# Feed-forward loop of a macaron block: both code planes of quantised x made by GpSimd instead of VectorE

## The reference

```
x = x + 0.5 * ffn(layernorm(x)); x = x + attn(layernorm(x)); x = x + 0.5 * ffn(layernorm(x))
ffn(x):  gate = q(x) @ q(w_gate).T; y = q(x) @ q(w_up).T; h = silu(gate) * y; return q(h) @ q(w_down).T
q(x):    per block of 16: scale = max|x| / 6; x / scale rounded to a grid of 8 magnitudes and sign, times scale
```

## Time and profile before

| what | us |
|---|---|
| median of three runs (lowest, highest) | 1416.26 (1414.32, 1421.88) |
| profiled execution, own time | 1417.98 |
| its span, first to last instruction | 1416.2 |
| busy in the span: TensorE, VectorE, ScalarE, GpSimd | 1258.7, 1160.1, 728.3, 578.6 |
| granted TensorE clock, mean | 0.981 of full |

### The profile page before, as it was taken

One profiled execution on the slowest core, in us unless ns is written; L12 is line 12 of the kernel. 1 busy time (PEld: TensorE's weight loads), 2 busy tenths in 40 slices (PEclk: granted clock), 3 DMA queues, 4 the chain that ended last, 5 costly groups with the idle time before them and its releaser, 6 DMA issues.

```text
span 1416.2 us, 28364 instructions
## 1 busy us (share of the span) xinstructions
PE 1258.7 (89%) x9008; PEld 820.2 (58%) x9008; DVE 1160.1 (82%) x3635; ACT 728.3 (51%) x1473; POOL 578.6 (41%) x530
## 2 busy tenths in 40 slices
PE   0669999999998699989998999899999999999997
PEld 0236555555555476767676677667755555555555
DVE  5689999999998686668667766676489999999997
ACT  3456666666653343424342443444276666666653
POOL 1144444445543244324332434244245444555542
PEclk9889999999999999999999999899999999999999
DMA  9524444444444000000000000000035444455555
GB/s 320 95 57 84 83 84 79 79 79 79 83 84 80 30 2 1 1 32 2 1 1 32 1 2 1 31 9 9 1 64 105 101 101 101 103 106 106 106 106 117
DMA packets 284583, 90.55 MB, mean 64 GB/s; under 512 B 263120, under 2 KB 283728, under 8 KB 284496
## 3 DMA queue, kind: packets, MB, share of 16 engines
q1 hardware_dynamic: 276752, 81.56, 27.9%
q10 hardware_dynamic: 7744, 7.86, 1.8%
HBM read 11.34 MB, written 8.39 MB: 14 GB/s over the span
## 4 chain that ended last, share of the span: by engine, by line
PE 31%; DVE 27%; issue 26%; POOL 8%; ACT 5%; DMA 1%; DVEq 1%; ACTq 0%; SPq 0%; POOLq 0%
PE ps L1378 12%; PE ps L1399 9%; DVE arena L833 4%; DVE arena L893 4%; POOL arena L461 4%; PE ps L1388 3%; PE ps L1358 3%; POOL arena L450 2%; DVE arena L837 2%; PE ps L1365 2%; DVE arena L822 2%; ACT arena L576 2%; ACT arena L615 2%; DVE arena L782 2%; DVE arena L846 1%
## 5 line engine op out<-in xcount | busy, mean ns | idle before, releaser
L1330 PE MATMUL ps<-wguT,arena 128*128 128x512 f16 (+1 forms) x2304 | 482.7, 364 | 26.4 <-DVE m_sb L1262 14.0
L1330 PEld LDWEIGHTS ps<-wguT,arena 128*128 128x128 f16 x2304 | 226.3, 98 | 251.2 <-issue 32.9
L461 POOL TENSOR_TENSOR arena<-arena 128x704 f32<-128x704 f32 x128 | 192.4, 1503 | 347.7 <-DVE arena L846 340.4
L1302 PE MATMUL ps<-wdT,arena 128*128 128x256 f16 x2176 | 262.3, 275 | 60.2 <-DMA arena<-arena 59.9
L1302 PEld LDWEIGHTS ps<-wdT,arena 128*128 128x128 f16 x2176 | 205.1, 98 | 125.1 <-issue 74.9
L483 POOL TENSOR_TENSOR arena<-arena 128x128 f16<-128x128 f32 (+7 forms) x64 | 143.9, 2249 | 239.0 <-ACT arena L680 239.0
L622 ACT ACTIVATE arena<-arena 128x704 int16<-128x704 f32 x128 | 100.8, 787 | 216.5 <-POOL arena L461 216.5
L1378 PE MATMUL ps<-arena 128*128 128x512 f16 (+2 forms) x960 | 194.1, 356 | 0.0
L1399 PE MATMUL ps<-arena 128*128 128x256 f16 x1632 | 191.8, 273 | 0.0
L672 ACT ACTIVATE arena<-ps,arena,cst 128x128 f32<-128x128 f32 (+7 forms) x64 | 80.4, 1257 | 183.9 <-DVE arena L1003 183.9
L1399 PEld LDWEIGHTS ps<-arena 128*128 128x128 f16 x1632 | 157.5, 98 | 22.7 <-issue 0.9
(11 more groups left out here) (126 smaller groups left out, 1675.2 us busy)
## 6 DMA issues: line engine op xcount, KB each, us to landing
out_dram<-x_sb SPq DMA_DIRECT2D x32, 256.0 KB, 2.7
x_sb<-in_L_attn_x_dram ACTq DMA_DIRECT2D x3, 2048.0 KB, 17.8
arena<-arena SPq DMA_TRANSPOSE x192, 3.5
arena<-arena SPq DMA_DIRECT2D x8, 256.0 KB, 2.8
arena<-arena SPq DMA_DIRECT2D x4, 512.0 KB, 4.2
x_sb<-in_L_attn_x_dram ACTq DMA_DIRECT2D x1, 1536.0 KB, 7.4
arena<-in_L_ffn_w_down_dram SPq DMA_DIRECT2D x1, 704.0 KB, 8.3
arena<-in_L_ffn_w_gate_dram SPq DMA_DIRECT2D x1, 640.0 KB, 4.5
```

Source lines behind the costliest of these rows:

```text
L461: g.tensor_tensor(hy[u].rearrange("p (j b) -> p b j", j=BL), h[u].rearrange("p (b j) -> p b j", j=BL), hri[u].unsqueeze(2).to_broadcast([P ...
L1302: i = nc.tensor.matmul(ps_dn[w % 2], hT[w][:, c * P:(c + 1) * P], wdT[:, k, :], start=(s == 0), stop=(s == len(DOWN_STEPS) - 1))
L1330: i = nc.tensor.matmul(psf[:, 1536 * u + lo:1536 * u + hi], xv[:, u, xl, kt, :], wguT[:, wl, lo // P:hi // P, kt, :], start=(s == 0), stop ...
```

## The change

GpSimd gets the two instructions that make `xq`. Its list of a pair becomes: `pool_h_y` first half, plane 0 of x, `pool_h_y` second half, plane 1 of x, `pool_x_y`, `pool_x_rstd`. VectorE loses both `dve_x_q` in the loop and keeps them for the first pairs of each phase, which are prepared in the head of the program and in the attention part. `x_q` now counts both planes (two for each pair), SyncE waits for `2 * q + 2`, and VectorE's `dve_x_sh` waits in addition until GpSimd has made both planes of the pair before, since it overwrites `xsh`. `act_*`, TensorE's list and the order of SyncE's list stay as they are.

```diff
         def sp_x_T(q, par):
-            nc.sync.wait_ge(x_q, q + 1)
+            nc.sync.wait_ge(x_q, 2 * q + 2)
...
+        def pool_x_q(q, pl, done=None):
+            g = nc.gpsimd
+            if pl == 0:
+                g.wait_ge(x_g, q + 1)
+                if done is not None:
+                    g.wait_ge(x_T[done[1]], done[0] * 16 + 16)
+            g.wait_ge((x_sh, x_sl)[pl], q + 1)
+            s = (xsh, xsl)[pl].rearrange("p (t b) -> p t b", t=2)
+            g.tensor_tensor(xq.rearrange("p (t l j b) -> p l t j b", t=2, l=2, j=BL)[:, pl],
+                            xg.rearrange("p (t j b) -> p t j b", t=2, j=BL),
+                            s.unsqueeze(2).to_broadcast([P, 2, BL, XB]), ALU.mult).then_inc(x_q, 1)
...
         def dve_x_sh(q):
             V.wait_ge(x_sd, q + 1)
+            if not isinstance(q, int) or q >= 1:
+                V.wait_ge(x_q, q * 2)
...
                 dve_h_sh(n, u)
-                if early:
-                    dve_x_q(gp + 2, 0, (qd + odd, 1 - odd))
                 dve_h_sl(n, u)
-                if early:
-                    dve_x_q(gp + 2, 1)
```

More of the change, by code:

```diff
@@ L501, in macaron_block_kernel, with pool_pair @@
         X_SLOT = (3, 6, 9, 12)
-        def pool_pair(gp, odd, x3=True, x4=True):
+        def pool_pair(gp, qd, odd, x2=True, x3=True, x4=True):
             pool_h_y(2 * gp, 0)
+            if x2:
+                pool_x_q(gp + 2, 0, (qd + odd, 1 - odd))
             pool_h_y(2 * gp + 1, 1)
+            if x2:
+                pool_x_q(gp + 2, 1)
             if x3:
@@ L553, in _ @@
                     continue
-                pool_pair(first, 0)
-                pool_pair(first + 1, 1)
+                pool_pair(first, first // 2, 0)
+                pool_pair(first + 1, first // 2, 1)
                 with pool.Fori(0, (NP - 6) // 2) as i:
-                    pool_pair(i * 2 + (first + 2), 0)
-                    pool_pair(i * 2 + (first + 3), 1)
+                    pool_pair(i * 2 + (first + 2), i + (first // 2 + 1), 0)
+                    pool_pair(i * 2 + (first + 3), i + (first // 2 + 1), 1)
                 for k in range(NP - 4, NP):
-                    pool_pair(first + k, k % 2, x3=(k < NP - 3), x4=(k < NP - 4))
+                    pool_pair(first + k, (first + k) // 2, k % 2, x2=(k < NP - 2), x3=(k < NP - 3), x4=(k < NP - 4))
                     if not first and k == NP - 3:
@@ L821, in dve_x_q @@
             s = (xsh, xsl)[pl].rearrange("p (t b) -> p t b", t=2)
[L822 to L826, removed]
+            V.tensor_tensor(xq.rearrange("p (t l j b) -> p l t j b", t=2, l=2, j=BL)[:, pl],
+                            xg.rearrange("p (t j b) -> p t j b", t=2, j=BL),
+                                s.unsqueeze(2).to_broadcast([P, 2, BL, XB]), ALU.mult).then_inc(x_q, 1)
         def dve_h(n, u):
```

## The result

The change makes the kernel slower: 1473.24 us (median of four runs, 1472.25 to 1476.35) against 1417.89 (1414.32 to 1421.88), ratio 1.0393, 95% interval 1.0359 to 1.0427. The forecast was 1462, with a range of 1403 to 1490.

What follows compares the result with a forecast made beforehand. It took the loop's path through VectorE, GpSimd and ScalarE as the bound. One stretch growing from 5.37 to 6.12 us gave +0.75 us a pair, times 60 pairs +45 us, so 1462 us, range 1403 to 1490.

Steps and rivals of the forecast that it cites:

- the give-back of the path ahead of GpSimd's recorded end: Path shared by VectorE and GpSimd: GpSimd gives it up about 0.14 us ahead of its instruction's end.
- The first rival: At plane 0 GpSimd loses the race, or little is lost: -14 us, far end -39 us; chance 0.17.
- the second: Rival: only plane 0 collides and `dve_x_s` is not held at plane 1: +0.17 us a pair, +10 us; chance 0.10.
- The third: Rival: GpSimd's planes hold the path from start to end: +1.09 us a pair, +65 us; chance 0.15.
- The other half of that reading: Path shared by VectorE and GpSimd: GpSimd needs it only from about 0.14 us behind its instruction's start.
- the 5.37 us: Stretch of a pair from the end of `dve_x_g` to the end of `pool_x_y`, forecast to become 6.12: +0.75 us.
- the rival walk in which nobody is held: Far end of the faster rival: small VectorE instructions never wait, `pool_x_y` ends at 4.72: -0.65 us a pair; chance 0.05.

Runs made afterwards that it cites:

- `tiny_planes`: The changed kernel, with each plane GpSimd makes in the loop cut to 4 of its 512 columns; waits and order kept: 1381.24 us, ratio 0.9722.
- `late_transpose`: The kernel before the change, with SyncE also waiting for the next pair's `pool_x_y` ahead of the transpose of x: 1423.91 us, ratio 1.0021.
- `plane0_after_hg`: The changed kernel, with GpSimd also waiting for `dve_h_g` of the same place ahead of plane 0: 1460.74 us, ratio 1.0291.
- `both_early`: Both planes on GpSimd between the two products of h, VectorE's x steps moved ahead of `dve_h_rin`: 1440.6 us, ratio 1.0139.
- `reorder_only`: The kernel before, planes on VectorE, with first-half `dve_x_sh`, `dve_x_c` and `dve_x_g` moved ahead of `dve_h_rin`: 1413.37 us, ratio 0.9959.

## Why the prediction was right

The direction and the mechanism were right, and the size was 10 us short: +55 us measured (58.4 between the two profiled executions) against +45. Point by point, in us from the end of `dve_x_g`, for the pair that was walked:

| step | predicted | measured |
|---|---|---|
| plane 0, start and end | 0.16, 1.29 | 0.23, 1.38 |
| `dve_h_rin` starts (1.29 before) | 1.50 | 1.60 |
| second product of h | 2.00 to 3.50 | 2.09 to 3.59 |
| plane 1 | 3.45 to 4.52 | 3.45 to 4.61 |
| `dve_x_s` comes, `dve_x_rin` starts | 3.79, 4.58 | 3.89, 4.68 |
| `pool_x_y` ends (5.37 before) | 6.12 | 6.18 |
| from there to the next end of `dve_x_g` | 6.70 | 6.69 |

Who goes first was called right at both places inside the loop: `dve_h_sl` still gets in, `dve_h_s` is held, `dve_x_s` is held. So was the give-back of the path ahead of GpSimd's recorded end: take its own 0.18 us off the end of `dve_h_s`, and it ran from 1247.77, 0.13 ahead of the plane's end; `dve_x_s`, with 0.17, ran from 1251.00, again 0.13 ahead. The first rival (GpSimd loses, faster) needed `dve_h_s` at 0.18 us and showed 1.16; the second (`dve_x_s` not held) was refuted at 0.76. (In that first walk `dve_x_s` comes at 2.92 and not at 2.96, which changes nothing.) The third (held from start to end) comes to 6.44 for the end of `pool_x_y` with the planes where they really ran: plane 0 until 1.38, `dve_h_rin` at 1.73, plane 1 until 4.74, `dve_x_rin` at 4.94 and 1.50 from there. Measured 6.18.

The other half of that reading, that GpSimd needs the path only from 0.14 us behind its start, isn't confirmed, and that `dve_h_sl` got in doesn't speak for it: plane 0 started at 0.23 and not at the predicted 0.16, so `dve_h_sl` at 0.15 was first in any case. Outside the loop plane 0 starts earlier, 0.07 to 0.09 behind `dve_x_g`, and there, in seven pairs, it is `dve_h_sl` (L897) that is held:

```profile
1078.72 1.16 POOL L464 TENSOR_TENSOR arena<-arena 128x512 f16<-128x512 f16 x1 [3.06 <-DVE arena L830]
1078.79 1.15 DVE L897 TENSOR_TENSOR arena<-arena 128x44 f16<-128x44 f32 x1
```

It starts 0.07 us behind the plane; if the plane left the path free for 0.14, it would have got in. In the loop, `dve_h_sl` is 0.08 ahead, and neither is longer for the 0.12 us in which their records overlap (0.20 and 1.15). So when GpSimd takes the path stays open. The sum hardly depends on it, since either order holds one short VectorE instruction until the plane ends.

Three terms were mis-sized. First, the walk came out 0.06 us short. Plane 0 started 0.07 later than predicted and ran 1.15 us where 1.13 had been reckoned (1.07 and a wait of 0.06), so the steps behind it came 0.09 to 0.10 late. Plane 1 took 1.16 in place of 1.07 (the f16 difference of attention in the earlier trace rows, 1.16, was the nearer row and not `pool_x_y`), but it started 0.14 ahead of the end of the product before it in place of 0.05, and so added nothing. And `pool_x_y` followed `dve_x_rin` 0.04 sooner than reckoned. Second, the 5.37 us are those of one half of the loop's body. In the other half the same stretch was 5.28 us (from 1214.52 to the end of `pool_x_y` at 1219.80), and it is 6.17 now. So one pair loses 0.81, the other 0.89, 0.85 on average, and 60 times that is 51 us. Third, the prediction said that the two `dve_x_q` were 0.86 us of the path; the rival walk in which nobody is held had `dve_h_rin` going from 1.29 to 0.63 without them, and `tiny_planes` shows 0.64. The right figure is 0.65, since one of them filled the time in which `dve_h_sl` waits for `dve_h_sh`. That sentence didn't enter the sum. Of the 58.4 us between the profiled executions 53.4 lie in the feed-forward phases, so 2 us there are left over, mostly in the pairs outside the loop; 4.1 lie in the attention part, where they differ from one execution to another, and 0.9 in the head.

TensorE behaved as told: it waits ahead of the gate product, 35.2 us in 23 waits of 2.0 us at most between 1100 and 1400 us, and no VectorE or ScalarE row shows the lateness. `late_transpose` shows that such waits are free here.

The Trainium skill, "SBUF — State Buffer", section "Who interferes with whom", has whoever issues first hold the path for the whole instruction. The exclusion agrees with every row above. By the recorded times the hold ends before the instruction does: a hold to the recorded end would have put the end of `pool_x_y` at 6.44, measured 6.18, and the held VectorE instruction goes some 0.13 us ahead of that end. "Whoever issues first" agrees with the recorded starts in the changed kernel, but not in the long pairs of `plane0_after_hg`: there `dve_x_s` has its start at 1275.60 and plane 1, at 1276.11, still goes before it.

## What to carry to other kernels

Before work is moved from VectorE to GpSimd, look not at GpSimd's idle time but at what VectorE runs in exactly that time: here GpSimd's long instructions ran freely beside reductions, products with one operand in PSUM, reciprocals (`dve_x_rin` keeps its 0.35 us beside plane 1 in `plane0_after_hg`) and tensor_scalars on one column; beside tensor_scalars on 31 columns and more and products with both operands in SBUF either engine stopped the other, and a stop of 1 us behind an instruction of 0.1 us costs more than the 0.42 us of the instruction that was moved. If the place collides, move VectorE's own small steps first, so that the moved instruction's inputs are ready where a harmless VectorE instruction runs; here the same plane cost 0.6 us a pair in one place and gained 0.18 in the other. A short instruction whose recorded duration jumps to that of its neighbour on the other engine is the mark to look for, since the busy shares count such waiting as work.

## What I had not expected of the hardware

- A VectorE instruction that waits behind GpSimd can be passed over: with the next GpSimd instruction queued right behind, `dve_x_s` was let in after 0.68 us in some pairs and after 1.70 us in others of the same execution (`plane0_after_hg`). What decides isn't shown. `both_early` has the same with `dve_h_q` and plane 1: either goes first, from pair to pair.
- A tensor_scalar of 31 f32 columns is held as one of 32 is (0.75 us against 0.76); the number being odd doesn't free it.
- VectorE stands still for some 0.2 to 0.3 us at the head of its loop's body, once in two pairs, already in the kernel before (0.31 us); the idle time ahead of `dve_h` is then missing in that pair, and I had counted on it in both in `reorder_only`.
